# Post-LN transformer layer on eight cores: LayerNorm finishes moved into the projection loop and the FFN, and the barrier between them taken out

## The reference

```python
# x: (4, 4096, 1024); Wq, Wk, Wv, Wo: (1024, 1024)
# w_gate, w_up: (3072, 1024); w_down: (1024, 3072), int32 in -127..127
x = layernorm(x + attention(x, Wq, Wk, Wv) @ Wo.T)
gate = x @ (w_gate / 127).T
up   = x @ (w_up / 127).T
x = layernorm(x + (silu(gate) * up) @ (w_down / 127).T)
# layernorm(v) = (v - mean(v)) / sqrt(var(v) + 1e-5), over the last axis
```

## Time and profile before

| | us |
|---|---|
| median of the 2 runs | 2086.98 |
| lowest and highest | 2084.97, 2088.98 |
| profiled execution, its own time | 2088.39 |
| its span on the slowest core (core 3) | 2087.3 |
| spans of the 8 cores | 2064.6 to 2087.3 |

### The profile page before, as it was taken

The page is one execution under the profiler, slowest core; times in us unless marked ns, Lnnn a source line. Parts: engine busy times, 40 slices in busy tenths (PEclk is TensorE's granted clock), DMA queues, the critical chain, the costliest instruction groups (busy, mean ns, idle before and its releaser), DMA issues. The chain is left out here.

```text
span 2087.3 us, 22783 instructions; the slowest of 8 cores (2064.6 to 2087.3 us)
## 1 busy us (share of the span) xinstructions
PE 1610.3 (77%) x7240; PEld 616.5 (30%) x7240; DVE 614.8 (29%) x1436; ACT 828.0 (40%) x999; POOL 183.6 (9%) x220
## 2 busy tenths in 40 slices
PE   3857988779888699987677656635999889998772
PEld 1512333223332133321111112212444333443320
DVE  1334233342332532325212212354111112111234
ACT  0025766657673576754377641321111011112003
POOL 1010000100001000000000000001222012221000
PEclk9977999879997699995588877767999999999895
DMA  7791233442332523240000005204779465776542
GB/s 99 109 135 23 41 55 48 62 71 42 52 56 37 72 43 60 41 62 2 2 1 1 1 2 126 66 10 41 71 71 91 46 66 51 75 75 67 86 71 81
DMA packets 223072, 115.31 MB, mean 55 GB/s; under 512 B 152014, under 2 KB 213456, under 8 KB 222960
## 3 DMA queue, kind: packets, MB, share of 16 engines
q0 software_dynamic: 214064, 96.94, 38.3%
q1 hardware_dynamic: 8896, 16.91, 2.5%
HBM read 201.66 MB, written 8.65 MB: 101 GB/s over the span
## 5 line engine op out<-in xcount | busy, mean ns | idle before, releaser
L415 ACT ACTIVATE pt<-sp,cbias 128x1024 bf16<-128x1024 f32 (+3 forms) x640 | 623.5, 986 | 360.0 <-PE sp L403 348.2
L443 PE MATMUL op<-pt,vbuf 128*65 128x512 bf16 (+3 forms) x1280 | 376.4, 379 | 124.9 <-DVE pt L424 55.1
L398 PE MATMUL sp<-qbuf,kbuf 64*128 64x512 bf16 (+3 forms) x640 | 238.5, 381 | 2.1 <-DVE cbias L324 2.1
L403 PE MATMUL sp<-qbuf,kbuf 64*128 64x512 bf16 (+3 forms) x640 | 238.7, 382 | 0.0
L802 PE MATMUL gps<-x1b,wgb 128*128 128x512 bf16 x768 | 184.7, 384 | 42.8 <-DMA wub<-wuT 36.2
L860 PE MATMUL dps<-hbuf,wdd 128*128 128x512 bf16 x768 | 179.5, 392 | 34.3 <-DVE y L871 33.1
L443 PEld LDWEIGHTS op<-pt,vbuf 128*65 128x65 bf16 x1280 | 121.4, 117 | 266.4 <-issue 222.4
L811 PE MATMUL ups<-x1b,wub 128*128 128x512 bf16 x768 | 182.6, 381 | 0.0
L226 PE MATMUL pp<-xstg,wkb 128*128 128x512 bf16 x512 | 150.8, 414 | 40.6 <-DMA xstg<-xfm 40.6
L819 ACT ACTIVATE sgb<-gps 128x512 bf16<-128x512 f32 x96 | 57.3, 597 | 308.9 <-PE gps L802 308.9
L240 PE MATMUL pp<-wvb,xstg 128*128 128x256 bf16 x1024 | 163.9, 280 | 0.6
(11 more groups left out here) (89 smaller groups left out, 1210.3 us busy)
## 6 DMA issues: line engine op xcount, KB each, us to landing
xstg<-xfm POOLq DMA_DIRECT2D x32, 1024.0 KB, 9.3
xstg<-xq POOLq DMA_DIRECT2D x16, 1024.0 KB, 8.4
wgb<-wgT POOLq DMA_DIRECT2D x48, 256.0 KB, 4.9
wub<-wuT POOLq DMA_DIRECT2D x48, 256.0 KB, 6.1
wdd<-wdT POOLq DMA_DIRECT2D x16, 768.0 KB, 9.6
xres<-xq SPq DMA_DIRECT2D x32, 256.0 KB, 3.4
yout<-y SPq DMA_DIRECT2D x4, 2048.0 KB, 6.9
wqb<-wqT POOLq DMA_DIRECT2D x4, 512.0 KB, 7.8
```

The lines of the kernel that those rows point to most:

```text
L398: nc.tensor.matmul(sp[buf][:, js * 128: 512], kbuf[pb][0:64, hp * T + kb * 128: hp * T + kb * 128 + 128], qbuf[pb][0:64, hp * TOWN + qbase ...
L403: s_s.inc(nc.tensor.matmul(sp[buf][:, 512 + js * 128: 1024], kbuf[pb][64:128, hp * T + kb * 128: hp * T + kb * 128 + 128], qbuf[pb][64:128 ...
L415: s_exp.inc(nc.scalar.activation(pview, sview, AF.Exp, bias=cbias[pb][:, 0:1]))
L443: lastpv = nc.tensor.matmul(ops[hl][:, js * 128: 512], vbuf[pb][:, kb * VGW + (2 * hp + hl) * 65: kb * VGW + (2 * hp + hl) * 65 + 65], pt[ ...
```

## The change

- **Order in the projection.** `stats_pe(s - 1)` now follows the iteration ncx = 2 of slice s, and `finish(s - 1)` the iteration ncx = 5. At the end of a slice only `stats_act(s)` stays.
- **`finish` in two parts.** `finish_rows` makes the rows, `finish_tail` does the broadcast and the 16 VectorE operations. For slices 0 to 2 they are called one behind the other. Behind the loop only `stats_pe(3)` is left. `finish_rows(3)` stands behind the x1b casts of the first half, `finish_tail(3)` ahead of the matmuls of hidden chunk 4.
- **Waits in place of the barrier.** The three waits for the last LayerNorm operation and the barrier are gone. At the start of the FFN, VectorE and GpSimd wait for the last projection matmul and the last eviction, and VectorE, before the casts of a half, for the apply of that half's last slice (slice 1 for the first half, 3 for the second).
- **Tiles.** ysq, ybf (8 each; ln1 had 16) and rows are allocated once and ln2 is ln1, with a new `ready_of`. The PSUM tiles gps and ups are allocated ahead of the projection's, so that they share no bank with it, and dps after wps is given up.
- The load of the Silu table stands behind `finish_rows(3)`.

```diff
@@ class LN
-            def finish(self, s):
+            def finish_rows(self, s):
...
-                nc.tensor.wait_ge(sV.h, sV.n)
+                self.rows_done = sV.n
+
+            def finish_tail(self, s):
+                sA, sV, sP = self.sA, self.sV, self.sP
+                sb = s % self.nst
+                bb = s % self.nbc
+                rows = self.rows
+                q0 = s * 512
+                nc.tensor.wait_ge(sV.h, self.rows_done)
                 nc.tensor.wait_ge(sV.h, self.apply_bc[bb])
                 nc.tensor.matmul(self.bc2[bb][0][:, :], ones_row_f[:, :],
                                  rows[:, 1024:1536], start=True, stop=True)
...
+            def finish(self, s):
+                self.finish_rows(s)
+                self.finish_tail(s)
@@ projection loop
+            if ncx == 2 and s >= 1:
+                ln1.stats_pe(s - 1)
+            if ncx == 5 and s >= 1:
+                ln1.finish(s - 1)
+                ln1_done[s - 1] = ln1.apply_st[(s - 1) % ln1.nst]
             if ncx == NCH - 1:
                 y_slice_done[s] = s_evV.n
                 ln1.stats_act(s)
-                if s >= 1:
-                    ln1.stats_pe(s - 1)
-                    if s >= 2:
-                        ln1.finish(s - 2)
+        wo_pe_done = s_prj.n
+        wo_dve_done = s_evV.n
         ln1.stats_pe(NQS - 1)
-        ln1.finish(NQS - 2)
-        ln1.finish(NQS - 1)
-        nc.tensor.wait_ge(s_lnV.h, s_lnV.n)
-        nc.scalar.wait_ge(s_lnV.h, s_lnV.n)
-        nc.vector.wait_ge(s_lnV.h, s_lnV.n)
...
-        nc.all_engine_barrier()
@@ FFN
+            if fs == 0:
+                nc.vector.wait_ge(s_prj.h, wo_pe_done)
+                nc.vector.wait_ge(s_evV.h, wo_dve_done)
+                nc.gpsimd.wait_ge(s_prj.h, wo_pe_done)
+                nc.gpsimd.wait_ge(s_evV.h, wo_dve_done)
+            hi = min((t0 + FFS) // 512 - 1, NQS - 1)
+            nc.vector.wait_ge(s_lnV.h, ln1_done[hi])
             for m in range(NCH):
                 s_fdve.inc(nc.vector.tensor_scalar_mul(
                     x1b[:, m * FFS:(m + 1) * FFS],
                     y[:, m * TOWN + t0: m * TOWN + t0 + FFS], cfg["QSCALE"]))
             x1b_ready = s_fdve.n
+            if fs == 0 and NFS >= 2:
+                ln1.finish_rows(NQS - 1)
+            if fs == 0:
+                preload_table_set(nc, "silu_and_others")
...
             for hc in range(NHC):
                 wi = hc % 2
+                if fs == 0 and NFS >= 2 and hc == 4:
+                    ln1.finish_tail(NQS - 1)
+                    ln1_done[NQS - 1] = ln1.apply_st[(NQS - 1) % ln1.nst]
```

More of the change, by code:

```diff
@@ L521, in build_program @@
         y = st.enter_context(nc.sbuf_tensor("y", [128, NCH * TOWN], F32))
+        ysq = [st.enter_context(nc.sbuf_tensor(f"ysq{i}", [128, 512], BF16))
+               for i in range(8)]
+        ybf = [st.enter_context(nc.sbuf_tensor(f"ybf{i}", [128, 512], BF16))
+               for i in range(8)]
+        rows = st.enter_context(nc.sbuf_tensor("rows", [1, 4 * 512], F32))
         ph_b = ExitStack()
@@ L525, in build_program @@
                 for i in range(4)]
[L526 to L533, removed]
+        ffn_ps = ExitStack()
+        gps = ffn_ps.enter_context(nc.psum_tensor("gps", [128, 512], F32))
+        ups = ffn_ps.enter_context(nc.psum_tensor("ups", [128, 512], F32))
         s_wo.inc(nc.gpsimd.dma_start(
@@ L595, in stats @@
                 self.stats_pe(s)
-            def finish(self, s):
+            def finish_rows(self, s):
                 sA, sV, sP = self.sA, self.sV, self.sP
                 sb = s % self.nst
-                bb = s % self.nbc
                 rows = self.rows
-                q0 = s * 512
                 nc.scalar.wait_ge(sP.h, self.stats_done[sb])
@@ L643, in build_program @@
                 for j in range(2)] for i in range(1)]
+        wo_ps = ExitStack()
+        wps = [wo_ps.enter_context(nc.psum_tensor(f"wps{i}", [128, 512], F32))
+               for i in range(2)]
         y_slice_done = [0] * NQS
+        ln1_done = [0] * NQS
         ln1 = LN(stp, bc2, ysq, ybf, rows, s_lnA, s_lnV, s_lnP,
@@ L689, in build_program @@
                 ln1.stats_act(s)
-                if s >= 1:
-                    ln1.stats_pe(s - 1)
-                    if s >= 2:
-                        ln1.finish(s - 2)
+        wo_pe_done = s_prj.n
+        wo_dve_done = s_evV.n
         ln1.stats_pe(NQS - 1)
-        ln1.finish(NQS - 2)
-        ln1.finish(NQS - 1)
-        nc.tensor.wait_ge(s_lnV.h, s_lnV.n)
-        nc.scalar.wait_ge(s_lnV.h, s_lnV.n)
-        nc.vector.wait_ge(s_lnV.h, s_lnV.n)
+        if NFS < 2:
+            ln1.finish(NQS - 1)
+            ln1_done[NQS - 1] = ln1.apply_st[(NQS - 1) % ln1.nst]
         ofm_st.close()
-        ln_ps.close()
         wo_ps.close()
         ph_b.close()
-        nc.all_engine_barrier()
         if debug:
+            nc.sync.wait_ge(s_lnV.h, s_lnV.n)
             s_out.inc(nc.sync.dma_start(dbg_y1, y[:, :]), 16)
@@ L718, in build_program @@
                for i in range(2)]
[L719 to L724, removed]
-        y2_slice_done = [0] * NQS
[L726 to L733, removed]
+        y2_slice_done = [0] * NQS
+        dps_st = ExitStack()
+        dps = [dps_st.enter_context(nc.psum_tensor(f"dps{i}", [128, 512], F32))
                for i in range(1)]
         sgb = ph_c.enter_context(nc.sbuf_tensor("sgb", [128, 512], BF16))
-        preload_table_set(nc, "silu_and_others")
         def load_gu(hc, wi):
@@ L762, in load_wd @@
             wdd_ready[i] = s_wd2[i].n
-        ln2 = LN(stpc, bcc, ysq2, ybf2, rows2, s_lnA, s_lnV, s_lnP,
-                 ready_of=lambda s: (s_fdve, y2_slice_done[s]))
+        ln2 = ln1
+        ln2.ready_of = lambda s: (s_fdve, y2_slice_done[s])
         def ln2_out(s):
@@ L878, in build_program @@
         nc.scalar.wait_ge(s_fdve.h, s_fdve.n)
-        ffn_ps.close()
         for sp_ in ln2_out_pending:
@@ L887, in build_program @@
         nc.scalar.wait_ge(s_lnV.h, s_lnV.n)
-        ln_ps2.close()
+        dps_st.close()
+        ln_ps.close()
+        ffn_ps.close()
         ph_c.close()
```

## The result

| | before | changed |
|---|---|---|
| median, us (10 and 11 executions) | 2091.5 | 2071.2 |
| ratio | | 0.9891, 95% interval 0.9865 to 0.9918 |
| span of the profiled execution, us | 2087.3 | 2065.7 |

What follows compares the result with a forecast made beforehand. TensorE's in-order stream was taken as the bound, with holes where VectorE normalises y. 31.4 gained less 9.4 lost gives 22.0 us off 2088.4, so 2066.4, or 2065.0 as median; range 2055 to 2076.

Steps and rivals of the forecast that it cites:

- Which resource sets the end: Around the edit, TensorE's in-order stream sets the end, with two long holes where VectorE normalises y.
- 4.0 us idle, then 15.8 us to resumption: Each finish in the projection loop: TensorE idles 4.0 us for the row chain, then 15.8 us from broadcast to resumption.
- T1: TensorE's resumption after slice 0's finish, inside slice 1 of the projection loop, put at 1327.0.
- Into the FFN, T3 + 9.3: First gate matmul 9.3 us after TensorE's resumption in slice 3, released by slice 3's statistics, at 1404.9.
- Gain of the first part, 31.4: First projection to first gate matmul: the first gate matmul comes at 1404.9 where it was 1436.28, gain 31.4 us.
- The tail, 9.4: Slice 3's broadcast and applies in chunk 4: stall and low-clock restart cost 10.8, less 1.37 weight wait, loss 9.4 us.
- The barrier at nothing beyond this: Removing the barrier at the end of the projection is worth nothing beyond the gain already counted.
- rival A: TensorE's clock stays high over the 4 us gaps before the broadcasts: 2060 us; chance 0.15.
- B: Chunk 4's stall costs up to 13 in place of 9.4, or the first load is 1.5 late: 2070; chance 0.10.
- C: Finishes in the projection loop cost what the one there costs today, ScalarE 8 us late at ncx 5: 2088; chance 0.06.
- D: After chunk 4's stall TensorE stays at 1.2 GHz through the gate/up stage: slower, up to 2192; chance 0.02.
- E: Whole kernel: a gain over 2%, needing more than 41.7 us; chance 0.04.

Runs made afterwards that it cites:

- tail spread: Changed kernel with slice 3's 16 VectorE operations put two behind each hbuf product over chunks 4 to 7; ratio to before 0.9863.
- all spread, tiles free early: Kernel with finishes' VectorE operations spread behind evictions, slice 3's in chunks 4 to 7, changed so each loop slice's last apply precedes the next rows; ratio to before 0.9681.
- Without a tail: Changed kernel with slice 3's broadcast and apply left out; first gate to first down matmul 176.0 us, ratio to before 0.9862.
- the rows early: Changed kernel with a finish's row operations called behind ncx 3, broadcast and applies still behind ncx 5; ratio to before 0.9834.

## Why the prediction was right

- **Which resource sets the end.** Right. The differences are in the two stretches named, and the one from first to last down matmul, which comes behind them, kept its length (411.7 to 413.8 us in all but two kernels). In these two it took 417.2 (tail spread) and 417.6 (all spread, tiles free early) in the median; in the second, four cores took 419 to 423 us and the other four 409 to 416. Why stays open.
- **4.0 us idle, then 15.8 us to resumption.** 4.05 three times; 15.8 at the first finish, and the same at the second (1347.75 to 1363.56). Reading them off the finish in the last down projection was the step that mattered: the finish in the old loop showed 11.71 instead.
- **Slice 1, T1 at 50.0 us after the first projection matmul.** It was 53.1. Some 1.3 us lie in slice 0, before anything has changed. 1.2 are a term that I left out: the last statistics pairs are spaced by ScalarE, TensorE is idle for 0.66 of every 1.04 us there, and the three groups behind them ran partly at low clock (6.58 us against 5.35 for those behind the next statistics). The last pair itself ended some 0.4 us later than I had it.
- **Into the FFN, T3 + 9.3.** It was T3 + 10.0. The three arrivals were close together as worked out, with the load last by 0.27.
- **Gain of the first part, 31.4.** It was 28.4, by these two terms. This is the term that was sized too large.
- **The tail, 9.4.** Without a tail the stretch is 9.8 shorter, and it rose by 10.6 over before. Of the sum, the 10.8 for the stall was near (10.0 less the weight waits), but the 1.37 us that I took off for weights doesn't show: the weight waits were 3.5 us before and 4.0 after. 14.0 us from broadcast to the next group (predicted 14.1), 6.8 idle (about 7), low clock after it.
- **The barrier at nothing beyond this.** The barrier by itself was nothing, as said. In the sum its removal lay inside the "into the FFN" step and is worth 8.5 there.
- **Clock, rival A.** On core 3 the broadcasts were at low clock in two of three cases and half in the third (1.09 then 1.82), close to the main case, which had all three low. By the Trainium skill ("TensorE: Matmul & The Clock Gate", section "HAM oscillation — how this bites in real kernels"), a loop whose wait in each turn is long enough pays the warm-up again in each turn. The rows agree for 18 of 24 broadcasts after 4.05 us; with the wait down to 0.61 us the pair took 1.09.
- **Rivals B to E.** B's late load didn't come (0.27 us). C needed ScalarE late at ncx 5; the idle time of 4.05 us excludes it. D: one low group after the stall, then 1.89. E: didn't occur.

The account by stretches gives 17.8 us and the prediction said 22.0. It was right in the mechanisms and some 4 us generous, and its two misses (3.0 us in the first part, 1.2 in the tail) go the same way. So it is luck that the profiled execution took 2066.7 us where 2066.4 were predicted: the earlier start of the projection, which isn't the edit's, stands in for 3.2 us of it. The prediction also took 2% for the least change that can be told from none. With an interval of 0.3% to either side, the 1.1% here can.

## What to carry to other kernels

When a normalisation stands between two matmul stages, moving it into the first stage's loop does nothing as long as it comes as one block in an in-order queue: 16.3 us a slice in the loop, 16.6 to 18.8 behind it. What helps is to give the next stage only what it needs (two slices of four), to let its loads start at the last use of their space and not at a barrier, and then to split the block into pairs that fit between evictions: 159.5 us went to 131.1, and to 91.9. Before moving such pieces, list each tile that they read, since the next writer waits for the last reader.

## What the runs showed of the hardware

- After 4.05 us without work, TensorE's granted clock was 1.2 GHz at the next matmul in 18 of the 24 broadcasts in the changed kernel's projection loop (2.04 us for the first pair, as at 1313.07 and 1347.75), and 2.4 GHz in 6 (1.09 to 1.20 us, then 1.66 to 1.91 for the second pair, as at 1382.44). With the rows early, after 0.61 us idle at most, it was 2.4 GHz in all 24 (1.09 to 1.12 us).
- The clock also fell around shorter pauses. In the kernel with all applies spread and the tiles free early, the broadcast in the FFN waits 2.40 us on each of the eight cores, and the group behind it takes 2.5 to 3.6 us in place of 1.89. In its loop, after 0.60 us idle, the broadcast at 1305.00 ran at high clock, but the 24 matmuls behind it took 7.04 us, against 5.35 behind the next one.
- It fell without any longer pause, too: in statistics pairs every 1.04 us, with 0.66 us idle between them, a matmul went from 0.38 us to 0.58 (1300.87 and 1301.91 in the changed kernel).
- The weight waits of one and the same gate/up stage differ by core from 1.7 to 12.4 us in one execution; a comparison of a single core would have shown the tail at 2.7 us (core 3, 182.3 to 185.0) and not at 10.
